# Second product of the expert network in three float32r passes, with its low halves from GpSimd

## Chip, cores and metric

One core of one Trainium2 chip. Metric: device time of one execution in microseconds (us), median of several runs.

## The reference

For 16 samples x[b] of 128 x 256 (channels by positions) and a context of the same shape:

```python
x = x + xattn(layernorm(x), ctx, ctx, gamma)     # 8 heads of 16 channels, softmax over 256 keys
x = x + ffn(layernorm(x), ...)

def ffn(x):                                       # H = 256
    top_expert = argmax(softmax(x @ Wg.T))
    out0 = gelu(x @ W0a.T + b0a) @ W0b.T + b0b    # hidden size 512
    out1 = relu(x @ W1a.T + b1a) @ W1b.T + b1b
    return where(top_expert == 0, out0, out1)
```

## The kernel before

Everything is float32 to the outside. Each engine runs its own instruction list, written out by hand; semaphores (`wait_ge`, `then_inc`) tie the lists together. All lists share one loop: `for n in range(-LEAD, SLOTS)` with LEAD = 7 and SLOTS = 64. A slot is one pair of heads of one sample: `b, j = divmod(n, 4)`, and `c, k = divmod(n + 7, 4)` is the sample whose row maxima are taken ahead.

**Attention.** q and k are split into a high part (ScalarE, `high`, rounded to float32r) and a low part (GpSimd, `low`); SP stacks them by DMA into `qkst` (`stacks`, 6 DMAs of 128 KB a sample). In each slot TensorE does the scores of sample b (`scores`, L654, into `st`) and the scores in the other layout for sample c (`maxima`, L642, into `smax`); ScalarE takes exp of `st` (`exp`, L513); VectorE takes the negated row maxima of `smax` (`take_max`, L358). `st` and `smax` have one buffer each: scores wait for the exp before, maxima for the take_max before. Once per sample the maxima are transposed, split (`copy_max`, `max_parts`) and put into `qkst` by two small DMAs (`max_rows`, L190); the first scores of that sample wait for them. `values` (32 matmuls, L666), `transpose_od` and `transpose_att` finish the attention. VectorE then makes x1 (`residual`), its moments, x_norm and the gate; GpSimd takes the inverse root (`rstd`, L239) and the expert masks.

**Expert network.** It runs on pairs of samples, i = 0 to 7, four samples behind the attention. A pair takes eight slots: an even and an odd value of b. There are 8 units of 128 hidden features: 0 to 3 are gelu, 4 to 7 relu. The first product (`gemm1`, L723) is already in three float32r passes: w high by x high, w high by x low, w low by x high, 6 matmuls of 256 columns a unit for both samples. The weights' high half is made by ScalarE (L576) and the low half by GpSimd (L309) at b = 2 and 3. `hidden` (L542) applies gelu or relu from PSUM bank `ff[:, u // 2 % 2]` into `hid`. The second product (`gemm2`, L740) multiplies `hid` by `w2t` in float32, 8 units a sample, in `ff[:, b % 2]`. `final` (L418 and L423) masks the two experts' outputs, adds x1 and makes y, and `gemm1` waits for y before it writes the same banks.

By slots, with b even: j = 0 gemm1 units 0 to 3; j = 1 the gelu units on ScalarE, behind exp; j = 2 gemm1 units 4 to 7 and the relu units; j = 3 gemm2 of sample b - 4, units 0 to 3. With b odd: j = 0 gemm2 of sample b - 5, units 4 to 7; j = 2 and 3 gemm2 of sample b - 4. `final` of the even sample stands on VectorE at j = 2 of odd b, that of the odd sample at j = 0 of the next even b, behind take_max. The first pair is at b = 4 and 5; the last two pairs of products (samples 12 to 15) stand behind the loop. Pairs 0 to 5 are in the loop.

**Start.** SP loads the samples, issues the stacks and the max rows, and in its iterations b = 0 and b = 1 also w1 and w2 (L225, L227).

Of the kernel before, what the change touches and what calls it, by code (L numbers as in the profile page):

```python
# [16 lines left out]
EXPERTS = 2  # L17
# [13 lines left out]
ROWS = STACK + 2  # L31
STACK_INC = 2 * len(Q_PART) * 16
# [13 lines left out]
X1 = 8  # L46


def build(nc, first, qkin, xvin, w1, w2, b1, b2, wg, gamma, out):
    with ExitStack() as stack:  # L50
# [28 lines left out]
        w2t = sb("w2t", [128, UNITS, L])  # L79
        b1t = sb("b1t", [128, UNITS])  # L80
# [8 lines left out]
        bias_r = sb("bias_r", [128, EXPERTS * L])  # L89
# [22 lines left out]
        hid = sb("hid", [128, UNITS, 2 * C])  # L112
        yt = sb("yt", [128, 2, L])
# [27 lines left out]
        s_g1, s_hid, s_g2 = sem("s_g1"), sem("s_hid"), sem("s_g2")  # L141
        s_y0, s_y = sem("s_y0"), sem("s_y")
# [21 lines left out]
        def _(sp):  # L164
# [50 lines left out]
            for b in range(B):  # L215
# [20 lines left out]
        def _(pool):  # L236
# [54 lines left out]
            for n in range(-LEAD, SLOTS):  # L291
                b, j = divmod(n, PAIRS)
                for c in prepared(n):
                    if c > 2:
                        rstd(c, mv1, c, s_var1, s_rstd1)
                    low(c)
# [8 lines left out]
                if j == 2 and b >= 2:  # L305
                    masks(b - 2)
                if b == 3 and j < LC:
# [8 lines left out]
        def _(dve):  # L316
# [96 lines left out]

            def final(b):
# [11 lines left out]
            def gate_and_bias(step):  # L426
# [6 lines left out]
                if step == 2:  # L433
                    dve.wait_ge(s_bias, 1)
                    dve.tensor_tensor(bias_r[:, :], bias_f[:, :], bias_p[:, 0, :], ALU.subtract).then_inc(s_bias, 1)
                if step == 3:
                    dve.wait_ge(s_bias, 2)
                    dve.tensor_copy(bias_p[:, 1, :], bias_r[:, :]).then_inc(s_bias, 1)
                if step == 4:
                    dve.wait_ge(s_bias, 3)  # L440
                    dve.tensor_tensor(bias_p[:, 2, :], bias_r[:, :], bias_p[:, 1, :], ALU.subtract).then_inc(s_bias, 1)
# [15 lines left out]
            for n in range(-LEAD, SLOTS):  # L457
                b, j = divmod(n, PAIRS)
                c, k = divmod(n + LEAD, PAIRS)
                if c == 0:  # L460
# [11 lines left out]
                if j == 0 and b >= 2:  # L472
                    if b >= 6 and b % 2 == 0:
                        final(b - 5)
# [27 lines left out]
        def _(act):  # L502
# [33 lines left out]

            def hidden(i, u):
                if u % 2 == 0:
                    act.wait_ge(s_g1, UNITS // 2 * i + u // 2 + 1)
                if u == 0 and i:  # L540
# [24 lines left out]
            for n in range(-LEAD, SLOTS):  # L565
                b, j = divmod(n, PAIRS)
                c, k = divmod(n + LEAD, PAIRS)
                if b >= 1:
# [12 lines left out]
                if j == 1 and b >= 4:  # L581
                    if b % 2 == 0:
                        if b == 4:
                            act.wait_ge(s_small, 64)
                        for u in range(4):
                            hidden((b - 4) // 2, u)
# [5 lines left out]
                if j == 3 and b >= 2:  # L592
                    high_xT(b - 2)
            for u in range(4):
# [10 lines left out]
        def _(pe):  # L605
# [121 lines left out]

            def gemm2(b, units):
                t = b % 2
                if 0 in units:  # L730
                    if b == 0:
                        pe.wait_ge(s_w2, 16)
                        pe.wait_ge(s_bias, 7)
                        pe.wait_ge(s_ones, 2)
                    pe.wait_ge(s_hid, UNITS * (b // 2) + (UNITS if t else UNITS - 2))
# [106 lines left out]
```

## Time and profile before

| | |
|---|---|
| Median of 3 runs | 268.23 us (266.91 to 270.09) |
| The profiled execution | 267.05 us |
| its span (first to last instruction) | 264.8 us |
| TensorE, weight loads, VectorE, ScalarE, GpSimd busy | 86%, 65%, 63%, 51%, 24% |
| mean granted TensorE clock | 0.972 of 2.4 GHz |
| HBM read, written | 11.28 MB, 2.10 MB |

The busy share by 40 slices of 6.6 us shows the three stages: a start of some 70 us in which TensorE is often idle and the DMA engines are full, pairs of samples to 230 us with TensorE at 9 tenths, and a tail.

```profile
PE   0748947869599999999999999999999989989995
...
DVE  3775687989635787578757875787476615333302
ACT  2014335665249454945494549554944494632230
...
DMA  4589999989712447375837582646202000000101
```

Each digit is tenths of a slice. Spans of matmuls overlap, so a busy TensorE need not be at its peak; the starts of matmuls tell its rate.

### The profile page before, as it was taken

How to read it: one execution, taken by the hardware profiler on the slowest of the kernel's cores; microseconds unless marked ns; L12 is line 12 of the kernel's file. 1: busy time of each engine (PE TensorE's matmuls, PEld its weight loads, DVE VectorE, ACT ScalarE, POOL GpSimd, SP SyncE). 2: the span in 40 equal slices, each digit the busy share in tenths (PEclk: the TensorE clock that was granted, in tenths of full speed). 3: DMA queues.
4: the chain of work that ended last, by engine and by line, in shares of the span. 5: the costliest groups of instructions: out<-in, count | busy, mean ns of one | idle time of the engine just before them, and what ended most of it. 6: DMA issues, size and time to landing. Idle time of an engine off the chain costs nothing.

```text
span 264.8 us, 4862 instructions
## 1 busy us (share of the span) xinstructions
PE 228.1 (86%) x1858; PEld 172.2 (65%) x1872; DVE 167.5 (63%) x348; ACT 134.7 (51%) x208; POOL 63.9 (24%) x112
## 2 busy tenths in 40 slices
PE   0748947869599999999999999999999989989995
PEld 0425524444478676867686768676867676869893
DVE  3775687989635787578757875787476615333302
ACT  2014335665249454945494549554944494632230
POOL 6592120335700431043104310431101011011000
PEclk9999999798779999999999999999999999999999
DMA  4589999989712447375837582646202000000101
GB/s 158 85 156 165 207 289 171 253 165 153 102 22 80 101 136 110 100 107 123 116 101 102 125 117 62 99 97 108 64 0 64 0 22 2 20 22 0 40 2 40
DMA packets 19562, 25.75 MB, mean 97 GB/s; under 512 B 2644, under 2 KB 13140, under 8 KB 19284
## 3 DMA queue, kind: packets, MB, share of 16 engines
q1 hardware_dynamic: 18312, 24.25, 46.7%
q10 hardware_dynamic: 1228, 1.19, 2.1%
q8 instruction: 15, 0.25, 0.5%
q14 instruction: 7, 0.06, 0.1%
HBM read 11.28 MB, written 2.10 MB: 51 GB/s over the span
## 4 chain that ended last, share of the span: by engine, by line
PE 58%; ACT 17%; DVE 9%; DMA 7%; issue 7%; POOL 0%; SPq 0%; ACTq 0%; DVEq 0%
PE ff L740 21%; PE ff L723 12%; PE st L654 8%; DMA qkst<-mlow 6%; PE od L666 6%; ACT P L513 5%; ACT hid L542 4%; PE smax L642 3%; ACT L542 3%; PE st L629 2%; PE od L674 2%; ACT L513 2%; DVE nmax L351 2%; DVE y L423 1%; DVE yt L418 1%
## 5 line engine op out<-in xcount | busy, mean ns | idle before, releaser
L513 ACT ACTIVATE P<-st 128x1024 f32<-128x1024 f32 x64 | 65.8, 1028 | 85.4 <-PE st L654 76.9
L358 DVE TENSOR_REDUCE nmax<-smax 128x4 f32<-128x1024 f32 x54 | 66.2, 1226 | 40.2 <-PE smax L642 38.9
L740 PE MATMUL ff<-w2t,hid 128*128 128x256 f32 x256 | 60.0, 379 | 1.5 <-issue 1.1
L740 PEld LDWEIGHTS ff<-w2t,hid 128*128 128x128 f32 x256 | 47.7, 190 | 5.8
L723 PE MATMUL ff<-xnTh,w1h 128*128 128x256 f32 x128 | 39.1, 306 | 9.0 <-DVE y L423 3.4
L239 POOL TENSOR_TENSOR mv<-mv,power 128x1 f32<-128x1 f32 x31 | 18.3, 591 | 103.8 <-DVE mv L323 103.8
L654 PE MATMUL st<-qkst 50*128 50x256 f32 x240 | 31.2, 339 | 9.1 <-DMA qkst<-mlow 5.5
L723 PE MATMUL ff<-xnTl,w1h 128*128 128x256 f32 x128 | 37.1, 290 | 0.0
L723 PE MATMUL ff<-xnTh,w1l 128*128 128x256 f32 x128 | 37.1, 290 | 0.0
L654 PEld LDWEIGHTS st<-qkst 50*128 50x128 f32 x240 | 18.5, 191 | 26.2 <-issue 14.4
L666 PE MATMUL od<-P,vt 128*32 128x256 f32 x512 | 33.5, 406 | 0.0
L723 PEld LDWEIGHTS ff<-xnTh,w1h 128*128 128x128 f32 x128 | 25.2, 197 | 12.1 <-DVE y L423 4.4
L244 POOL TENSOR_TENSOR parts<-qk,parts 128x512 fp32r<-128x512 f32 x14 | 17.8, 1274 | 62.1 <-ACT parts L507 62.0
L542 ACT ACTIVATE hid<-ff,b1t 128x256 f32<-128x256 f32 x64 | 25.5, 479 | 9.7 <-PE ff L723 9.6
L723 PEld LDWEIGHTS ff<-xnTl,w1h 128*128 128x128 f32 x128 | 25.3, 197 | 0.0
L723 PEld LDWEIGHTS ff<-xnTh,w1l 128*128 128x128 f32 x128 | 25.2, 197 | 0.0
L666 PEld LDWEIGHTS od<-P,vt 128*32 128x32 f32 x512 | 15.8, 117 | 14.0 <-issue 6.0
L642 PE MATMUL smax<-qkst 48*128 48x256 f32 x216 | 24.2, 304 | 0.0
L642 PEld LDWEIGHTS smax<-qkst 48*128 48x128 f32 x216 | 18.2, 203 | 2.5 <-issue 1.3
L418 DVE SCALAR_TENSOR_TENSOR yt<-ff,mask,x 128x256 f32<-128x256 f32 x16 | 7.6, 474 | 11.5 <-PE ff L740 11.5
L412 DVE TENSOR_TENSOR xnTl<-tr,xnTh 128x256 fp32r<-128x256 f32 x16 | 6.7, 421 | 11.7 <-ACT xnTh L534 11.7
L507 ACT ACTIVATE parts<-qk 128x512 fp32r<-128x512 f32 x14 | 8.9, 639 | 9.0 <-DVE qk L347 9.0
(73 smaller groups left out, 250.9 us busy)
## 6 DMA issues: line engine op xcount, KB each, us to landing
qkst<-parts SPq DMA_DIRECT2D x87, 128.0 KB, 4.7
xv<-in_xv SPq DMA_DIRECT2D x16, 256.0 KB, 2.9
qk<-in_qk SPq DMA_DIRECT2D x15, 256.0 KB, 4.6
out<-y SPq DMA_DIRECT2D x16, 128.0 KB, 2.4
w1t<-in_w SPq DMA_DIRECT2D x1, 1024.0 KB, 10.2
w2t<-in_w SPq DMA_DIRECT2D x1, 1024.0 KB, 9.9
qkst<-parts ACTq DMA_DIRECT2D x3, 128.0 KB, 6.2
qk<-in_first SPq DMA_DIRECT2D x1, 256.0 KB, 3.4
```

The lines of the kernel that those rows point to most:

```text
L239: pool.tensor_tensor(mv[:, b % 2, 11:12], mv[:, b % 2, 10:11], power[:, 0:1], ALU.pow).then_inc(s_rstd, 1)
L244: pool.tensor_tensor(parts[:, c % 2, 0:4:3, :], qk[:, place(c, QK), :, :], parts[:, c % 2, 1:3, :], ALU.subtract).then_inc(s_lo, 1)
L358: dve.tensor_reduce(nmax[:, c % 2, :, :, j].rearrange("p a e -> p e a"), (ff if c in WIDE and j % 2 else smax)[:, :, :, :], AX.X, ALU.max, ...
L418: dve.scalar_tensor_tensor(out=yt[:, t, :], in0=ff[:, t, 0, :], scalar=mask[:, b % X1, 0:1], in1=x1[:, b % X1, :], op0=ALU.mult, op1=ALU.a ...
L507: act.activation(parts[:, c % 2, 1:3, :], qk[:, place(c, QK), :, :], ACT.Copy).then_inc(s_hi, 1)
L513: act.activation(P[:, b % 2, j, :, :, :].rearrange("p e a l -> p (e a l)"), st[:, :, :, :].rearrange("p e a l -> p (e a l)"), ACT.Exp, sca ...
L542: act.activation(hid[:, u, :], ff[:, u // 2 % 2, u % 2, :], ACT.Gelu if u < HM else ACT.Relu, bias=b1t[:, u:u + 1]).then_inc(s_hid, 1)
L642: mm = pe.matmul((ff if wide and j % 2 else smax)[:, e, a, :], qkst[rows, s, j, 0, a * 128:(a + 1) * 128], qkst[rows, s, j, 1, :], start=T ...
L654: mm = pe.matmul(st[:, e, a, :], qkst[rows, s, j, 1, a * 128:(a + 1) * 128], qkst[rows, s, j, 0, :], start=True, stop=True)
L666: mm = pe.matmul(od[32 * j:32 * j + 32, e * L:(e + 1) * L], vt[:, b % 2, HEADS * a + PAIRS * e + j, :], P[:, b % 2, j, e, a, :], start=a = ...
L723: mm = pe.matmul(ff[:, u // 2 % 2, u % 2, :], w[:, a, e, m * 128:(m + 1) * 128], xs[:, i % 2, a, :], start=a == 0 and n == 0, stop=a == LC ...
L740: mm = pe.matmul(ff[:, t, u // HM, :], hid[:, u, t * C:(t + 1) * C], w2t[:, u, :], start=False, stop=u == UNITS - 1)
```

## The change

For samples 0 to 11 (the six pairs in the loop) the second product goes in three float32r passes too. `hid` is split as x and w1 are: the high half of the gelu units by VectorE (`high_gelu`, a copy to float32r of 128 x 1024), that of the relu units by ScalarE (`high_relu`), both low halves by GpSimd (`low_hidden`, a subtraction of 128 x 1024 each). w2 is split in the same way at b = 3. A unit has three matmuls: hid high by w2 high and by w2 low (`high_pass`), hid low by w2 high (`low_pass`). The four samples behind the loop keep `gemm2` in float32.

Order, beside that: the gelu units stand ahead of exp in their slot on ScalarE; `final` of the odd sample stands ahead of take_max on VectorE; `low` of q and k stands two slots later on GpSimd; the even sample's last low pass, and so its final sum, comes in slot j = 2 of odd b. w1 and w2 are loaded by DMAs that ScalarE issues at n = 0 and n = 4. Buffers: X1 goes from 8 to 6, bias_r is gone; two new tiles for w2 and two for hid.

```diff
@@ SP
-                if b == 0:
-                    sp.dma_start(w1t[:, :, :, :].rearrange("p a e f -> p (a e f)"), w1).then_inc(s_w1, 16)
-                if b == 1:
-                    sp.dma_start(w2t[:, :, :].rearrange("p u l -> p (u l)"), w2).then_inc(s_w2, 16)
@@ GpSimd
+            def low_hidden(i, e):
+                pool.wait_ge((s_hidHg, s_hidHr)[e], i + 1)
+                units = slice(e * HM, (e + 1) * HM)
+                pool.tensor_tensor(hidL[:, units, :], hid[:, units, :], hidH[:, units, :], ALU.subtract).then_inc(s_hidL, 1)
...
+                if j == 0 and b >= 5 and b % 2:
+                    low_hidden((b - 5) // 2, 1)
+                if b >= 4 and j == 3 and b % 2 == 0:
+                    low_hidden((b - 4) // 2, 0)
+                for c in prepared(n - 2 if n > 0 else n) if n else ():
                     low(c)
...
+                if b == 3 and j >= 2:
+                    pool.wait_ge(s_w2h, j - 1)
+                    half = slice((j - 2) * HM, (j - 1) * HM)
+                    pool.tensor_tensor(w2l[:, half, :], w2t[:, half, :], w2h[:, half, :], ALU.subtract).then_inc(s_w2l, 1)
@@ VectorE
+            def high_gelu(i):
+                dve.wait_ge(s_hid, UNITS * i + HM)
+                if i:
+                    dve.wait_ge(s_g2, 2 * i)
+                dve.tensor_copy(hidH[:, 0:HM, :], hid[:, 0:HM, :]).then_inc(s_hidHg, 1)
...
+                if j == 0 and b >= 6 and b % 2 == 0:
+                    final(b - 5)
                 if c == 0:
                     take_max0(k)
...
+                if j == 2 and b >= 4 and b % 2 == 0:
+                    high_gelu((b - 4) // 2)
@@ ScalarE
+            def high_relu(i):
+                act.wait_ge(s_hid, UNITS * (i + 1))
...
+                act.activation(hidH[:, HM:UNITS, :], hid[:, HM:UNITS, :], ACT.Copy).then_inc(s_hidHr, 1)
...
+                if j == 1 and b >= 4:
+                    if b % 2 == 0:
...
+                        for u in range(4):
+                            hidden((b - 4) // 2, u)
                 if b >= 1:
                     exp(b, j)
...
+                if n == 0:
+                    act.dma_start(w1t[:, :, :, :].rearrange("p a e f -> p (a e f)"), w1).then_inc(s_w1, 16)
+                if n == PAIRS:
+                    act.dma_start(w2t[:, :, :].rearrange("p u l -> p (u l)"), w2).then_inc(s_w2, 16)
...
+                if b == 3 and j < 2:
+                    act.wait_ge(s_w2, 16)
+                    half = slice(j * HM, (j + 1) * HM)
+                    act.activation(w2h[:, half, :], w2t[:, half, :], ACT.Copy).then_inc(s_w2h, 1)
@@ TensorE
+            def high_pass(b, e):
+                pe.wait_ge((s_hidHg, s_hidHr)[e], b // 2 + 1)
...
+                for u in range(e * HM, (e + 1) * HM):
+                    for w in (w2h, w2l):
+                        pe.matmul(ff[:, t, e, :], hidH[:, u, t * C:(t + 1) * C], w[:, u, :], start=False, stop=False)
+            def low_pass(b, e):
+                pe.wait_ge(s_hidL, EXPERTS * (b // 2) + e + 1)
...
                 if j == 0:
...
                     if odd:
-                        gemm2(b - 5, range(4, 8))
+                        low_pass(b - 5, 0)
+                        high_pass(b - 5, 1)
                 if j == 2:
...
                     if odd:
-                        gemm2(b - 4, range(0, 4))
+                        low_pass(b - 5, 1)
+                        begin(b - 4)
+                        high_pass(b - 4, 0)
+                        low_pass(b - 4, 0)
...
                 if j == 3 and b >= 1:
...
                     if even:
-                        gemm2(b - 4, range(0, 4))
+                        begin(b - 4)
+                        high_pass(b - 4, 0)
                     if odd:
-                        gemm2(b - 4, range(4, 8))
+                        high_pass(b - 4, 1)
+                        low_pass(b - 4, 1)
```

`hidden` also waits for hidL of the pair before instead of s_g2, which lets it overwrite `hid` earlier; `begin` is the bias matmul that stood in gemm2.

Three places as the instructions stand there. First TensorE, the odd sample's first slot, behind its maxima (b = 7; od<-identf,attT is a transpose of the attention's output). Before:

```order
L642 MATMUL smax<-qkst 128x256 [waits s_max]
L642 MATMUL smax<-qkst 128x256 x3
L681 MATMUL od<-identf,attT 128x128 [waits s_attT]
L681 MATMUL od<-identf,attT 128x128
L740 MATMUL ff<-w2t,hid 128x256 x2
L740 MATMUL ff<-w2t,hid 128x256 [waits s_hid]
L740 MATMUL ff<-w2t,hid 128x256
```

And now:

```order
L688 MATMUL smax<-qkst 128x256 [waits s_max]
L688 MATMUL smax<-qkst 128x256 x3
L727 MATMUL od<-identf,attT 128x128 [waits s_attT]
L727 MATMUL od<-identf,attT 128x128
L796 MATMUL ff<-w2h,hidL 128x256 [waits s_hidL]
L796 MATMUL ff<-w2h,hidL 128x256 x3
L790 MATMUL ff<-w2h,hidH 128x256 [waits s_hidHr]
L790 MATMUL ff<-w2l,hidH 128x256
```

Four float32 units, of which the first two wait for nothing new, gave way to a low pass of the gelu units that waits for GpSimd (s_hidL) and a high pass of the relu units that waits for ScalarE (s_hidHr).

Second ScalarE, the second slot of an even sample (b = 6); P<-st is exp, mhigh<-tr the transposed maxima's high part. Before:

```order
L513 ACTIVATE P<-st 128x1024 [waits s_sc]
L525 ACTIVATE mhigh<-tr 8x256 [waits s_mT,s_mst0]
L542 ACT_TABLE_LOAD [waits s_g2]
L542 ACTIVATE hid<-ff,b1t 128x256 [waits s_g1]
L542 ACTIVATE hid<-ff,b1t 128x256
L542 ACTIVATE hid<-ff,b1t 128x256 [waits s_g1]
L542 ACTIVATE hid<-ff,b1t 128x256
L513 ACT_TABLE_LOAD
L513 ACTIVATE P<-st 128x1024 [waits s_sc]
L530 ACTIVATE ods<-od 128x512 [waits s_pv]
```

And now:

```order
L578 ACT_TABLE_LOAD [waits s_hidL]
L578 ACTIVATE hid<-ff,b1t 128x256 [waits s_g1]
L578 ACTIVATE hid<-ff,b1t 128x256
L578 ACTIVATE hid<-ff,b1t 128x256 [waits s_g1]
L578 ACTIVATE hid<-ff,b1t 128x256
L538 ACT_TABLE_LOAD
L538 ACTIVATE P<-st 128x1024 [waits s_sc]
L550 ACTIVATE mhigh<-tr 8x256 [waits s_mT,s_mst0]
L538 ACTIVATE P<-st 128x1024 [waits s_sc]
L555 ACTIVATE ods<-od 128x512 [waits s_pv]
```

Table load, four units and the load back moved from between two exps to ahead of both; the first load waits for s_hidL in place of s_g2.

Third GpSimd at b = 3, from the slot j = 0; parts<-qk,parts is `low`, vt<-xv a padded copy of v. Before:

```order
L239 TENSOR_TENSOR mv<-mv,power 128x1 [waits s_var2]
L309 TENSOR_TENSOR w1l<-w1t,w1h 128x1024 [waits s_w1h]
L239 TENSOR_TENSOR mv<-mv,power 128x1 [waits s_var1]
L244 TENSOR_TENSOR parts<-qk,parts 128x2x256 [waits s_hi]
L309 TENSOR_TENSOR w1l<-w1t,w1h 128x1024 [waits s_w1h]
L257 COPY vt<-xv 128x16x16 [waits s_pv,s_xv0]
L262 TENSOR_SCALAR mask<-lead 128x1 [waits s_lead]
L262 TENSOR_SCALAR mask<-lead 128x1
```

And now:

```order
L241 TENSOR_TENSOR mv<-mv,power 128x1 [waits s_var2]
L326 TENSOR_TENSOR w1l<-w1t,w1h 128x1024 [waits s_w1h]
L241 TENSOR_TENSOR mv<-mv,power 128x1 [waits s_var1]
L326 TENSOR_TENSOR w1l<-w1t,w1h 128x1024 [waits s_w1h]
L259 COPY vt<-xv 128x16x16 [waits s_pv,s_xv0]
L270 TENSOR_SCALAR mask<-lead 128x1 [waits s_lead]
L270 TENSOR_SCALAR mask<-lead 128x1
L323 TENSOR_TENSOR w2l<-w2t,w2h 128x1024 [waits s_w2h]
L246 TENSOR_TENSOR parts<-qk,parts 128x2x256 [waits s_hi]
L323 TENSOR_TENSOR w2l<-w2t,w2h 128x1024 [waits s_w2h]
```

`low` went from ahead of the second half of w1l to behind the masks, and the two halves of w2l came in around it.

## Rows read from the trace of the kernel before

**Rows 1.** The page: busy time by engine; the chain that ended last, by engine.
```profile
PE 228.1 (86%) x1858; PEld 172.2 (65%) x1872; DVE 167.5 (63%) x348; ACT 134.7 (51%) x208; POOL 63.9 (24%) x112
...
PE 58%; ACT 17%; DVE 9%; DMA 7%; issue 7%; POOL 0%; SPq 0%; ACTq 0%; DVEq 0%
```

**Rows 2.** Chain of waits, whole span: start us, length us, what was being worked on.
```profile
101.04 1.71 PE ff L723 x12
...
207.56 1.71 PE ff L723 x12
```

**Rows 3.** Timeline of TensorE, one pair: start us, length us, engine, line, operation, count.
```profile
126.95 0.28 PE L723 MATMUL ff<-xnTh,w1l 128*128 128x256 f32 x1
127.68 0.39 PE L723 MATMUL ff<-xnTh,w1h 128*128 128x256 f32 x1 [0.45 <-DVE y L423]
...
129.32 0.51 PE L654 MATMUL st<-qkst 50*128 50x256 f32 x4
...
132.17 0.50 PE L654 MATMUL st<-qkst 50*128 50x256 f32 x4
132.51 0.40 PE L642 MATMUL smax<-qkst 48*128 48x256 f32 x4
133.34 0.39 PE L723 MATMUL ff<-xnTh,w1h 128*128 128x256 f32 x1 [0.43 <-ACT hid L542]
...
136.29 0.38 PE L706 MATMUL tr<-identf,xn 128*128 128x128 f32 x2
...
137.98 1.89 PE L740 MATMUL ff<-w2t,hid 128*128 128x256 f32 x8
139.80 0.51 PE L654 MATMUL st<-qkst 50*128 50x256 f32 x4
```

**Rows 4.** Timeline of ScalarE, the same pair.
```profile
131.15 1.28 ACT L542 ACT_TABLE_LOAD   x1
132.45 1.57 ACT L542 ACTIVATE hid<-ff,b1t 128x256 f32<-128x256 f32 x4
134.03 1.28 ACT L513 ACT_TABLE_LOAD   x1
135.33 1.03 ACT L513 ACTIVATE P<-st 128x1024 f32<-128x1024 f32 x1
```

**Rows 5.** Timeline of VectorE, the same pair.
```profile
137.39 1.23 DVE L358 TENSOR_REDUCE nmax<-smax 128x4 f32<-128x1024 f32 x1 [2.57 <-PE smax L642]
```

**Rows 6.** Groups by line, shapes apart: count, busy us, mean ns, idle before.
```profile
L740 PEld LDWEIGHTS ff<-w2t,hid 128*128 128x128 f32 x256 | 47.7, 190 | 5.8
...
L309 POOL TENSOR_TENSOR w1l<-w1t,w1h 128x1024 fp32r<-128x1024 f32 x2 | 4.7, 2349 | 0.0
...
L397 DVE TENSOR_SCALAR xn<-x,mv 128x256 f32<-128x256 f32 x16 | 7.2, 447 | 2.1 <-POOL mv L239 2.1
...
L438 DVE CAST bias_p<-bias_r 128x512 bf16<-128x512 f32 x1 | 0.6, 634 | 0.0
```

**Rows 7.** Chain of waits, the first 76 us.
```profile
30.85 5.37 DMA qkst<-mlow
...
41.01 5.61 DMA qkst<-mlow
...
68.16 2.51 issue
70.67 5.40 PE ff L723 x24
```

**Rows 8.** Timeline of GpSimd (POOL), the first 76 us.
```profile
61.01 2.36 POOL L309 TENSOR_TENSOR w1l<-w1t,w1h 128x1024 fp32r<-128x1024 f32 x1
...
68.23 2.34 POOL L309 TENSOR_TENSOR w1l<-w1t,w1h 128x1024 fp32r<-128x1024 f32 x1
```

**Rows 9.** Timeline of VectorE (DVE), the first 76 us.
```profile
62.52 1.00 DVE L397 TENSOR_SCALAR xn<-x,mv 128x256 f32<-128x256 f32 x1
```

**Rows 10.** One stretch of 2 us by engine, with clock, DMA share, GB/s.
```profile
36.00:38.00 2.00, 1.22 (x8) 0.93 (x8) 0.83 (x2) 0.90 (x1) 0.61 (x2) 1.00 1.02 419
```

More of the change, by code:

```diff
@@ L31 @@
 ROWS = STACK + 2
+LAST = B // 2 - 2
 STACK_INC = 2 * len(Q_PART) * 16
@@ L45 @@
 XV = 4
-X1 = 8
+X1 = 6
 def build(nc, first, qkin, xvin, w1, w2, b1, b2, wg, gamma, out):
@@ L79, in build @@
         w2t = sb("w2t", [128, UNITS, L])
+        w2h = sb("w2h", [128, UNITS, L], F32R)
+        w2l = sb("w2l", [128, UNITS, L], F32R)
         b1t = sb("b1t", [128, UNITS])
@@ L88, in build @@
         bias_f = sb("bias_f", [128, EXPERTS * L])
-        bias_r = sb("bias_r", [128, EXPERTS * L])
         bias_p = sb("bias_p", [128, 3, EXPERTS * L], BF16)
@@ L112, in build @@
         hid = sb("hid", [128, UNITS, 2 * C])
+        hidH = sb("hidH", [128, UNITS, 2 * C], F32R)
+        hidL = sb("hidL", [128, UNITS, 2 * C], F32R)
         yt = sb("yt", [128, 2, L])
@@ L141, in build @@
         s_g1, s_hid, s_g2 = sem("s_g1"), sem("s_hid"), sem("s_g2")
+        s_hidHg, s_hidHr, s_hidL, s_w2h, s_w2l = map(sem, ("s_hidHg", "s_hidHr", "s_hidL", "s_w2h", "s_w2l"))
         s_y0, s_y = sem("s_y0"), sem("s_y")
@@ L472, in _ @@
                 if j == 0 and b >= 2:
-                    if b >= 6 and b % 2 == 0:
-                        final(b - 5)
                     residual(b - 2)
@@ L535, in high_xT @@
                                ACT.Copy).then_inc(s_xTh, 1)
+            def high_relu(i):
+                act.wait_ge(s_hid, UNITS * (i + 1))
+                if i:
+                    act.wait_ge(s_g2, 2 * i)
+                act.activation(hidH[:, HM:UNITS, :], hid[:, HM:UNITS, :], ACT.Copy).then_inc(s_hidHr, 1)
             def hidden(i, u):
@@ L539, in hidden @@
                     act.wait_ge(s_g1, UNITS // 2 * i + u // 2 + 1)
-                if u == 0 and i:
+                if u % HM == 0 and 0 < i < LAST:
+                    act.wait_ge(s_hidL, EXPERTS * (i - 1) + u // HM + 1)
+                if u == 0 and i == LAST:
+                    act.wait_ge(s_hidL, EXPERTS * LAST)
+                if u == 0 and i > LAST:
                     act.wait_ge(s_g2, 2 * i)
@@ L567, in _ @@
                 c, k = divmod(n + LEAD, PAIRS)
+                if j == 1 and b >= 4:
+                    if b % 2 == 0:
+                        if b == 4:
+                            act.wait_ge(s_small, 64)
+                        for u in range(4):
+                            hidden((b - 4) // 2, u)
                 if b >= 1:
@@ L580, in _ @@
                     copy_max(c - 1)
[L581 to L586, printed above, removed]
                 if j == 2 and b >= 1:
@@ L593, in _ @@
                     high_xT(b - 2)
+                    if b >= 4 and b % 2 == 0:
+                        high_relu((b - 4) // 2)
             for u in range(4):
@@ L726, in gemm1, with begin @@
                     mm.then_inc(s_g1, 1)
+            def begin(b):
+                t = b % 2
+                if b == 0:
+                    pe.wait_ge(s_w2, 16)
+                    pe.wait_ge(s_bias, 7)
+                    pe.wait_ge(s_ones, 2)
+                pe.wait_ge(s_hid, UNITS * (b // 2) + (UNITS if t else UNITS - 2))
+                pe.matmul(ff[:, t, :, :], onesb[:, :], bias_rows[:, :], start=True, stop=False)
+            def high_pass(b, e):
+                t = b % 2
+                pe.wait_ge((s_hidHg, s_hidHr)[e], b // 2 + 1)
+                if b == 0:
+                    pe.wait_ge(s_w2l, EXPERTS)
+                for u in range(e * HM, (e + 1) * HM):
+                    for w in (w2h, w2l):
+                        pe.matmul(ff[:, t, e, :], hidH[:, u, t * C:(t + 1) * C], w[:, u, :], start=False, stop=False)
+            def low_pass(b, e):
+                t = b % 2
+                pe.wait_ge(s_hidL, EXPERTS * (b // 2) + e + 1)
+                for u in range(e * HM, (e + 1) * HM):
+                    mm = pe.matmul(ff[:, t, e, :], hidL[:, u, t * C:(t + 1) * C], w2h[:, u, :],
+                                   start=False, stop=u == UNITS - 1)
+                if e == EXPERTS - 1:
+                    mm.then_inc(s_g2, 1)
             def gemm2(b, units):
@@ L730, in gemm2 @@
                 if 0 in units:
[L731 to L735, printed above, removed]
-                    pe.matmul(ff[:, t, :, :], onesb[:, :], bias_rows[:, :], start=True, stop=False)
+                    begin(b)
                 for u in units:
```

6 lines of the change are left out of this document (3 added, 3 removed).

## Prediction, written before the changed kernel ran

> **What bounds the kernel now.** I read the page first. TensorE is busy for 86% of the span and carries 58% of the chain that ended last; no other engine has over 63% [rows 1]. An average over stages does not say where a saving counts, so I next read the chain in order of time. From 101.04 to 207.56 us it shows the same pattern four times, once per pair of samples: 106.5 / 4 = 26.63 us a pair [rows 2]. Two further pairs, at b = 4, 5 and b = 14, 15, have nearly the same pattern; ahead of them lies a start of 70 us, behind them a tail of 35 us.
>
> Inside one pair I read TensorE's timeline [rows 3] by starts, because its spans overlap. Let T be the start of the even sample's first scores. A pair reaches from T to the next T, and the odd sample of this pair begins at 139.80 us. TensorE stands still in two places only. Before the matmul at 127.68 it waits for y, the final sum of the odd sample before: the previous start is 126.95 and starts are 0.12 apart, so 0.61 us are lost (0.45 by the profile's own count). Before 133.34 it waits for the first gelu units: from 132.51 the four maxima take 0.33 us, so 0.50 are lost. All else is back to back. So in these pairs nearly every microsecond taken from TensorE is a microsecond of the span, as long as the other engines keep up.
>
> **The second product.** Before, a block of four units in float32 takes from 137.98 to 139.80, 1.82 us or 0.455 us a unit [rows 3]. A pair has four such blocks (two samples of eight units), 7.28 us. In three float32r passes a unit costs three matmuls of the form that the first product has already: 24 of them take from 133.34 to 136.29, 0.123 us each [rows 3], 0.369 us a unit. 48 matmuls are 5.90 us. Saving: 1.4 us a pair; I take 1.3, as the float32 blocks that a transpose follows are a little shorter than 1.82.
>
> The Trainium skill ("FP8 and Floating Point Precision", TensorE Precision Notes) says that true FP32 takes 4 passes through the array. By that rule three passes cost three quarters, 0.341 us for 0.455, and the pair would save 1.8 us instead of 1.4. No row here has 0.114 us for a float32r matmul; the sum goes by 0.123.
>
> **The gelu units ahead of exp.** At the even sample's second slot ScalarE now does load table, four gelu units, load table, and only then the exp that the next scores wait for. Before, the exp came first. The first load now hides behind the first product. With the wait for y gone, the first product's last unit ends 0.61 us sooner, so the scores of row 129.32 start at 128.71 and the units 2 and 3 can be taken from about 128.9. Two units are half of 1.57 [rows 4], 0.79; load and start-up 1.30 (134.03 to 135.33); exp 1.03: done at 132.03. TensorE wants to start the next scores 0.61 us ahead of 132.17, at 131.56. It waits until 132.07. So the wait for y mostly becomes a wait for exp: of 0.61 us 0.10 is left. The wait of 0.50 before 133.34 goes, since units 0 and 1 are long done. Both together: 0.6 us a pair.
>
> **The new operations and their cover.** Per pair and expert there is one copy to the high half and one subtraction, of 128x1024.
> - ScalarE's copy (relu half): an exp of this size is 1.03 us [rows 4]. It stands after the last exp and xnTh of the even sample, and I place its end at 139.6, some 1.2 us after TensorE starts the odd sample. The high pass that needs it starts after scores, maxima, a transpose and a low pass, 1.4 us after that start. It just fits; if it is 0.5 us late, TensorE loses 0.3.
> - VectorE's copy (gelu half): VectorE stands idle for 2.57 us at that place, its next maximum waiting for the first product to pass [rows 5]. A cast of half the size takes 0.634 us [rows 6], so this one 1.27 at most, and it costs nothing. Without that cover it would be 1.2 us a pair.
> - GpSimd's two subtractions: 2.35 us each [rows 6], 4.7 us a pair on an engine at 24% [rows 1]. Gelu half: starts about 135.9, done 138.3, needed in the odd sample's first slot. Relu half: done about 142.0, needed at 144.3, two slots on. Both are covered, the first by 1 us. Behind them in GpSimd's queue stand the low halves of sample c (needed six slots on) and a one-column power for layer norm, which VectorE reads 1.5 us later.
> - VectorE's final sum now stands ahead of take_max in the even slot. It waits only for the pass just issued, and its 1 us delays a maximum that no one waits for there.
>
> Walking the pair with these numbers gives 24.7 us for 26.6: gain 1.9 a pair (1.3 + 0.6). The four pairs between the rows 2 and the pair b = 14, 15 give 5 x 1.9 = **9.5 us**. The last four samples keep the float32 form and the tail moves as it is.
>
> **The first pair.** It has no wait for y, and its table load must wait for the first product, so exp costs more: gain 1.3 + 0.5 - 0.8 = **1.0 us**.
>
> **The start.** Four things change.
> - Before, TensorE waits 2.51 us at 68.16 [rows 7]. That wait, which the chain calls issue, is for w1l: GpSimd's second half ran 68.23 to 70.57, queued behind the low halves of a sample that themselves waited for ScalarE [rows 8]. Now the low halves come later in the queue, the second half starts at about 64 and ends before TensorE asks. Gain 2.5.
> - Moved, it runs beside VectorE's TENSOR_SCALAR over 128x256. In the first half's time such an op took 1.00 us, where the mean of its group is 0.447 [rows 6], and it ended just after GpSimd did [rows 8, 9]. Now the normalising of q meets that, and ScalarE has two w2h copies of 1.03 more. Together up to 0.9 us on the chain through attT. Loss 0.9.
> - The loads of w1 and w2, 1 MB each, go on ScalarE's queue, about 5 us before their old places. At 419 GB/s one takes 2.5 us [rows 10]. The small max rows wait behind what is in flight: 5.37 and 5.61 us from issue to landing [rows 7], so w1 now delays the first of them by up to 2.5 us and w2 the second. But the same megabyte is gone from the time after it, when SP's queue was full as well, and by the third max rows most is given back. I take 1.2 lost; bounds 0 and 2.9.
> - After the 2.5 us of idling the 24 matmuls at 70.67 ran 0.213 us apart, 5.40 us in all [rows 7], for 2.95 at full clock [rows 3]: the granted clock had fallen to 1.2 GHz. Without the idle time I expect about half of that, 1.1 us; bounds 0 and 2.4.
>
> Start: 2.5 - 0.9 - 1.2 + 1.1 = **1.5 us**.
>
> On the queues the Trainium skill ("DMA: Bandwidth & Descriptors", DMA queue model) says that each DMA engine round-robins between the rows of queues, so ScalarE's queue does not stand behind SP's. No run here shows it. Strictly FIFO service would make the cost 0 and the time 1.2 us less.
>
> **Sum.** 9.5 + 1.0 + 1.5 = 12.0 us. The profiled execution took 267.05 us; that makes 255.05. The median of the runs shown is 1.2 us above it, so 256.2 against the median. I give 255.5.
>
> **Rivals.**
> - *The start keeps its gain or loses more.* With DMA free and the clock up the sum is 12 + 1.2 + 1.3 + 0.9, about 15.4: 252 us. With 2.9 lost, no clock regained and another 1.5 from idle gaps it is 7.7: 260 us. For the second speaks that the DMA engines have nothing idle even while the big loads run: their share is 1.02 [rows 10]. Chance 0.12 each.
> - *The subtraction arrives late in each pair.* If hidL or hidH comes 1 us later than I placed it, say because the gelu order pushes ScalarE's chain past the odd sample's start, five pairs give back 5 to 6 us: 261 us. Against: covers of 1 us and more in three of four places. Chance 0.10.
> - *The other side: weight loads.* A float32 unit has two weight loads, the three passes have three, and a load's span is 190 ns [rows 6]. If loads did not hide behind matmuls of 256 columns, a unit would cost 3 x 0.19 = 0.57 for 0.455, and 96 units lose 11 us for the 7.8 gained: 268 + 11 - (12 - 7.8) = 275 us. It decides from 0.5 us a unit on, at which the other gains are used up. Against: the first product has the same loads and comes out at 0.123. Chance 0.03.
> - *The change does little*, because VectorE takes over: it is at 63% of the span [rows 1], but in the odd sample I count 10.8 us of work for it from its timeline, against 11.0 for TensorE. If each of its slots were 0.4 us longer the pair would stay near 26.3 and the time near 264. Chance 0.03.
>
> **Numbers.** My forecast, 253 to 259 us, has 0.60. Time 255.5, range 251 to 261. A measurement of this kernel tells about 1% from no change: 2.7 us. Faster by over 1% 0.94, within 1% 0.02, slower 0.04.
>
> **What would show it.** Starts of equal matmuls 24.7 us apart from pair to pair. Each high pass of eight matmuls about 0.98 us. No wait for y before unit 2 of the first product; a wait of about 0.5 us for exp before the even sample's third scores. No 2.5 us gap before the first product; w1l's second half ending by 67 us. The first max rows landing 2 us later. Wrong would be: waits of TensorE on hidL or hidH, a lower granted clock inside the pairs, or float32r matmuls further apart than 0.13 us.

## The result, and the profile after

The changed kernel takes 256.85 us (median of 4, 256.7 to 258.24) against 268.5 us for the kernel before (median of 4): ratio 0.956, 95% interval 0.952 to 0.960. The profiled execution took 256.82 us (before 267.05), its span 255.0 us (before 264.8). The forecast was 255.5, range 251 to 261. The total is right; inside it one stage came out with the other sign.

The page after has a line of busy times and one of the chain by engine, like [rows 1]:

```profile
PE 221.7 (87%) x1968; PEld 171.4 (67%) x1968; DVE 170.5 (67%) x354; ACT 143.6 (56%) x216; POOL 97.0 (38%) x126
...
PE 71%; DVE 10%; ACT 8%; DMA 5%; issue 4%; POOL 0%; DVEq 0%; ACTq 0%
```

GpSimd has gone from 64 to 97 us of work and still stands nowhere on the chain; TensorE's part of the chain rose from 58% to 71%. The work was moved to an engine that had room.

Where the 9.8 us of span come from is read by the start of TensorE's scores (L654 before, L700 now), which close every stage:

| stage (b = sample) | before | after | gained | forecast |
|---|---|---|---|---|
| start, to the second scores of b = 4 | 76.00 | 76.35 | -0.35 | 1.5 |
| first pair, to b = 6 | 22.07 | 21.53 | 0.5 | 1.0 |
| four pairs, b = 6 to 14 | 106.52 | 99.16 | 7.4 | 7.6 |
| last pair and tail, from b = 14 | 60.2 | 58.0 | 2.2 | 1.9 |

**Inside a pair.** The chain of waits after, to be read against [rows 2] (start us, length us): the same group of 24 matmuls stands at

```profile
99.00 2.85 PE ff L769 x24
...
173.38 2.85 PE ff L769 x24
```

with two more between, so (173.38 - 99.00) / 3 = 24.79 us a pair, for 26.63 before. TensorE's timeline after, at the places of [rows 3] (start us, length us, then what it waited for, if anything):

```profile
126.36 0.28 PE L769 MATMUL ff<-xnTh,w1l 128*128 128x256 f32 x1
126.57 0.50 PE L700 MATMUL st<-qkst 50*128 50x256 f32 x4
...
129.91 0.50 PE L700 MATMUL st<-qkst 50*128 50x256 f32 x4 [0.42 <-ACT P L538]
...
137.14 0.73 PE L796 MATMUL ff<-w2h,hidL 128*128 128x256 f32 x4
137.70 0.28 PE L790 MATMUL ff<-w2h,hidH 128*128 128x256 f32 x1
...
138.54 0.28 PE L790 MATMUL ff<-w2l,hidH 128*128 128x256 f32 x1
138.75 0.50 PE L700 MATMUL st<-qkst 50*128 50x256 f32 x4
...
142.27 0.73 PE L796 MATMUL ff<-w2h,hidL 128*128 128x256 f32 x4
```

The waits for y and for hid are gone, one for exp has come, and eight matmuls of the high pass lie 0.12 apart (137.70 to 138.54 is seven steps). Their operands, as the timelines of ScalarE, VectorE and GpSimd show them for this pair:

```profile
136.15 1.08 ACT L566 ACTIVATE hidH<-hid 128x1024 fp32r<-128x1024 f32 x1
...
132.49 0.67 DVE L435 CAST hidH<-hid 128x1024 fp32r<-128x1024 f32 x1
...
133.25 2.39 POOL L265 TENSOR_TENSOR hidL<-hid,hidH 128x1024 fp32r<-128x1024 f32 x1 [2.48 <-DVE hidH L435]
...
137.33 2.39 POOL L265 TENSOR_TENSOR hidL<-hid,hidH 128x1024 fp32r<-128x1024 f32 x1
```

The gelu low half is done at 135.64 and needed at 137.14 (cover 1.5 us); the relu low half at 139.72 and needed at 142.27 (2.5 us); ScalarE's high half at 137.2 and needed at 137.70. That last cover, 0.5 us, is the thin one.

**The start.** The chain of waits over the first 85 us, against [rows 7]:

```profile
31.37 8.42 DMA qkst<-mlow
...
73.42 1.59 PE ff L769 x12
...
81.07 3.04 PE ff L769 x24
```

The issue of 2.51 us (a wait of TensorE, for w1l) has gone, and so has the second DMA of 5.61; but the first is 8.42 us long in place of 5.37. The first product ran at full clock: this stretch view has us, busy us by engine (TensorE, weight loads, VectorE, ScalarE, GpSimd), granted clock, DMA share, GB/s.

```profile
70.00:76.00 6.00, 5.45 (x44) 4.42 (x45) 5.51 (x11) 4.05 (x6) 6.00 (x7) 1.00 0.35 106
```

VectorE and GpSimd in the same stretch, against [rows 8, 9]:

```profile
67.31 0.99 DVE L414 TENSOR_SCALAR xn<-x,mv 128x256 f32<-128x256 f32 x1
...
70.20 0.97 DVE L364 TENSOR_SCALAR qk<-qk,mv 128x256 f32<-128x256 f32 x1
```

```profile
65.80 2.36 POOL L326 TENSOR_TENSOR w1l<-w1t,w1h 128x1024 fp32r<-128x1024 f32 x1
...
68.67 2.36 POOL L326 TENSOR_TENSOR w1l<-w1t,w1h 128x1024 fp32r<-128x1024 f32 x1
```

The three samples behind the first rows show a second loss. From the first scores of b = 1 to those of b = 4 they take 10.67, 10.83 and 10.27 us, for 10.41, 10.46 and 9.41 before: 1.5 us more in all, although no scores of b = 2 and 3 wait for max rows any more. The values blocks (32 matmuls between a sample's second and third scores) grew from 2.77, 2.73 and 2.67 us to 3.58, 3.28 and 3.25, 1.9 us in all. The block of b = 3 as a stretch, columns as above, before and after:

```profile
60.53:63.20 2.67, 2.67 (x33) 1.15 (x32) 2.60 (x6) 0.52 (x2) 2.67 (x2) 0.68 1.16 122
```

```profile
65.02:68.27 3.25, 3.25 (x33) 1.38 (x32) 3.17 (x7) 1.00 (x2) 3.00 (x3) 0.56 1.16 123
```

The granted clock is 0.56 where it was 0.68 (at b = 2, 0.55 for 0.67); at a clock of 1.00, inside the pairs, the same block takes 1.87 us. And ahead of that block TensorE now waits for VectorE's maximum:

```profile
64.07 0.50 PE L688 MATMUL smax<-qkst 48*128 48x256 f32 x4 [0.55 <-DVE nmax L375]
```

### The profile page after: what moved, and what is told of

Same layout as the page of the kernel before. It is cut to its first block, busy times and chain, and to the rows that moved or that the text cites. A ratio compares the mean times of both kernels' runs of the same rounds, so it can differ in the third digit from the quotient of the medians.

```text
span 255.0 us, 5113 instructions
## 1 busy us (share of the span) xinstructions
PE 221.7 (87%) x1968; PEld 171.4 (67%) x1968; DVE 170.5 (67%) x354; ACT 143.6 (56%) x216; POOL 97.0 (38%) x126
## 4 chain that ended last, share of the span: by engine, by line
PE 71%; DVE 10%; ACT 8%; DMA 5%; issue 4%; POOL 0%; DVEq 0%; ACTq 0%
PE ff L769 17%; PE od L712 9%; PE ff L790 9%; PE st L700 9%; PE ff L796 5%; PE ff L808 5%; PE smax L688 5%; ACT P L538 4%; DMA qkst<-mlow 3%; PE od L720 3%; DVE nmax L375 3%; PE st L675 2%; ACT hid L578 2%; PE od L727 2%; DVE nmax L368 2%
## 5 line engine op out<-in xcount | busy, mean ns | idle before, releaser
L700 PE MATMUL st<-qkst 50*128 50x256 f32 x240 | 31.3, 340 | 13.2 <-ACT P L538 6.7
L769 PE MATMUL ff<-xnTh,w1h 128*128 128x256 f32 x128 | 37.5, 293 | 1.2 <-DVE y L446 1.2
L700 PEld LDWEIGHTS st<-qkst 50*128 50x128 f32 x240 | 18.7, 193 | 27.9 <-ACT P L538 10.2
L578 ACT ACTIVATE hid<-ff,b1t 128x256 f32<-128x256 f32 x64 | 26.8, 471 | 16.7 <-PE ff L769 16.5
L769 PE MATMUL ff<-xnTl,w1h 128*128 128x256 f32 x128 | 35.9, 281 | 0.0
L265 POOL TENSOR_TENSOR hidL<-hid,hidH 128x1024 fp32r<-128x1024 f32 x12 | 28.6, 2387 | 18.5 <-DVE hidH L435 14.1
L712 PE MATMUL od<-P,vt 128*32 128x256 f32 x512 | 35.5, 424 | 0.0
L790 PE MATMUL ff<-w2h,hidH 128*128 128x256 f32 x96 | 26.6, 310 | 0.0
L688 PE MATMUL smax<-qkst 48*128 48x256 f32 x216 | 24.2, 304 | 0.9 <-DVE nmax L375 0.8
L769 PEld LDWEIGHTS ff<-xnTl,w1h 128*128 128x128 f32 x128 | 24.1, 188 | 0.0
L790 PE MATMUL ff<-w2l,hidH 128*128 128x256 f32 x96 | 23.9, 283 | 0.0
L688 PEld LDWEIGHTS smax<-qkst 48*128 48x128 f32 x216 | 18.0, 201 | 3.5 <-issue 1.8
L790 PEld LDWEIGHTS ff<-w2l,hidH 128*128 128x128 f32 x96 | 18.2, 190 | 0.3
L790 PEld LDWEIGHTS ff<-w2h,hidH 128*128 128x128 f32 x96 | 18.1, 189 | 0.1
```

The source lines that it names most:

```text
L265: pool.tensor_tensor(hidL[:, units, :], hid[:, units, :], hidH[:, units, :], ALU.subtract).then_inc(s_hidL, 1)
L578: act.activation(hid[:, u, :], ff[:, u // 2 % 2, u % 2, :], ACT.Gelu if u < HM else ACT.Relu, bias=b1t[:, u:u + 1]).then_inc(s_hid, 1)
L688: mm = pe.matmul((ff if wide and j % 2 else smax)[:, e, a, :], qkst[rows, s, j, 0, a * 128:(a + 1) * 128], qkst[rows, s, j, 1, :], start=T ...
L700: mm = pe.matmul(st[:, e, a, :], qkst[rows, s, j, 1, a * 128:(a + 1) * 128], qkst[rows, s, j, 0, :], start=True, stop=True)
L712: mm = pe.matmul(od[32 * j:32 * j + 32, e * L:(e + 1) * L], vt[:, b % 2, HEADS * a + PAIRS * e + j, :], P[:, b % 2, j, e, a, :], start=a = ...
L769: mm = pe.matmul(ff[:, u // 2 % 2, u % 2, :], w[:, a, e, m * 128:(m + 1) * 128], xs[:, i % 2, a, :], start=a == 0 and n == 0, stop=a == LC ...
```

## Experiments

The theory after this reading had three parts. In the pairs, the product gives about 1.1 us, and the two orders (gelu units ahead of exp, final sum ahead of the maximum) each about 0.7. In the start, the two weight loads issued early take away what the missing issue gives. And GpSimd's order, not the loads, removed that issue. The rivals: the second queue as such delays the small rows; one of the orders is worth nothing; the product brings all of it. All kernels are the changed one with one part edited; ratios are to the kernel before of the same batch, against 0.956 for the changed kernel.

### Weight loads back on SP's queue

```diff
-                if n == 0:  act.dma_start(w1t ..., w1)
-                if n == PAIRS:  act.dma_start(w2t ..., w2)
+                if b == 0:  sp.dma_start(w1t ..., w1)      # behind load_xv(b + 2)
+                if b == 1:  sp.dma_start(w2t ..., w2)
```

> The changed kernel with the loads of w1 and w2 back on SP's queue at b = 0 and b = 1. Changed kernel: ratio to before 0.956, span 255.0 us. Theory A (from the changed kernel's trace: the first max rows land 8.42 us after their issue, against 5.37 before, and TensorE never gets the time back; its landmarks at the third and fourth sample stay 3.7 us late): span 251.3 us, ratio 0.943, first max rows within 5.6 us, and waits for max rows again at the second and third sample. Theory B (prediction's term: the delay is mostly given back, 1.2 us lost): span 253.8, ratio 0.952. Theory C (the delay is in the number of DMA bytes before the row, not the queue, and moves to the next sample): span 255, ratio 0.956.

Measured: 255.42 us, ratio 0.950 [0.943, 0.956], span 254.2. Chain of waits:

```profile
31.43 6.09 DMA qkst<-mlow
...
42.32 5.85 DMA qkst<-mlow
...
53.52 5.37 DMA qkst<-mlow
```

The first max rows take 2.3 us less than in the changed kernel, but now the slots wait for the second and third too, as before. Of the lead (first scores of b = 4 at 69.54 for 71.61) most is lost again in the first product: two stretches, columns as above,

```profile
70.00:72.00 2.00, 1.64 (x11) 1.36 (x10) 1.97 (x5) 1.17 (x2) 2.00 (x2) 0.68 0.23 80
72.00:74.00 2.00, 2.00 (x12) 2.00 (x11) 1.47 (x5) 0.00 (x0) 2.00 (x2) 0.50 0.43 104
```

show a granted clock of 1.2 GHz, and the second scores of b = 4 come 6.02 us behind the first, for 4.74. In the 3 us ahead of that product TensorE's longest wait is 0.24 us. So the span is only 0.8 us shorter, and this run alone does not tell the place in time from the queue.

### The same loads later, still on ScalarE's queue

```diff
-                if n == 0:
+                if n == 2:
                     act.dma_start(w1t ..., w1)
-                if n == PAIRS:
+                if n == PAIRS + 2:
                     act.dma_start(w2t ..., w2)
```

> The changed kernel with the same two loads still on ScalarE's queue, but two slots later (n = 2 and n = 6), behind the issue of the max rows. If the place in time is what costs (theory A): first max rows land within 5.6 us again, span 251 to 252, ratio 0.943 to 0.947, like the run with SP's queue. If it is the second queue itself that delays SP's packets: the first max rows land in time, but the second ones, whose stacks share the DMA engines with w1, land 2.5 us late, span 254 to 255, ratio 0.952 to 0.956.

Measured: 253.41 us, ratio 0.945 [0.938, 0.951], span 251.0. The issue of w1 moved from 25.9 to 32.0 us, that of w2 from 40.7 to 44.1. The chain of waits and the stretch with the first product:

```profile
31.00 5.66 DMA qkst<-mlow
```

```profile
68.00:72.00 4.00, 3.61 (x30) 3.21 (x29) 3.49 (x9) 2.11 (x3) 4.00 (x3) 1.00 0.27 70
```

This is the run that decides. The queue is the same as in the changed kernel, only the time differs, and the first rows take 2.8 us less. All four of the microseconds are in the start: the second scores of b = 4 stand at 72.34 for 76.35, and all later stages are equal to within 0.05 us. In the run before this one w1 went out at 32.5 us, from the other queue, and the rows took 6.09. So the time of issue costs, not the queue. An early issue from SP's queue was not tried. (0.4 of the four are a first load of 3.56 us for 3.93, which no edit touches.)

The lead also grows after the first rows, from 3.1 us at b = 1 to 4.0 at b = 3. All of that 0.9 is in the values blocks of b = 1 to 3, which take 9.20 us together for 10.11; for b = 3 the granted clock is 0.61 for 0.56. The w2 load is 3.4 us later too, and I did not take the two apart.

### GpSimd's low halves of q and k at their old place

```diff
+                    if n < 15:
+                        low(c)       # behind the power of sample c, as before
...
-                for c in prepared(...): low(c)
+                for c in prepared(...):
+                    if n > 16:
+                        low(c)
```

> The changed kernel with GpSimd's low halves of q and k, up to b = 3, back in their old slot, ahead of the second half of w1l. Theory A: TensorE waits about 2.5 us before its first product again and the 24 matmuls behind that wait run 0.213 us apart (granted clock at 1.2 GHz), so the span is 4.2 us longer: 259.2 us, ratio 0.972. Theory B: with ScalarE's copies of w2 and the later start the wait is there, but the clock stays up: 2.0 us longer, 257, ratio 0.963. Theory C: w1l is not what TensorE waited for: no change.

Measured: 260.78 us, ratio 0.972 [0.965, 0.979], span 260.9. Chain of waits:

```profile
74.94 2.52 issue
77.46 5.47 PE ff L772 x24
```

The wait of [rows 7] comes back to 0.01 us and the half clock with it: 5.47 us for 24 matmuls. Two terms of the start, 2.5 and the clock, hang on this one reorder, and it is not the weight loads that brought them. The run also prices the meeting of VectorE and GpSimd, for here the normalising of q has GpSimd idle beside it:

```profile
71.91 0.40 DVE L367 TENSOR_SCALAR qk<-qk,mv 128x256 f32<-128x256 f32 x1
```

It takes 0.40 us where the changed kernel takes 0.97. Yet the sample of b = 3 is as long as there (10.31 us for 10.27), and TensorE is ready for its first product 1.61 us after the first scores of b = 4 (73.33 to 74.94), where it is 1.70 us in the changed kernel (71.61 to 73.31). So the meeting costs 0.1 us. (The first max rows of this run took 9.06 us to land, 0.6 more than in the changed kernel; that is no part of the reorder's price.)

### The final sum behind the maximum again

```diff
-                if j == 0 and b >= 6 and b % 2 == 0:
-                    final(b - 5)           # ahead of take_max
...
                 if j == 0 and b >= 2:
+                    if b >= 6 and b % 2 == 0:
+                        final(b - 5)
                     residual(b - 2)
```

> The changed kernel with the final sum of the odd sample back behind take_max on VectorE. Theory A: the wait for y of 0.6 us a pair returns ahead of unit 2 of the first product, and the wait for exp (0.42 us a pair) stays, since exp moves with the units: 5 x 0.6 = 3.0 us longer, span 258.0, ratio 0.967. Theory B: the wait for exp absorbs it, since exp is then the later of the two: 0.5 to 1 us longer, ratio 0.958 to 0.960.

Measured: 260.60 us, ratio 0.971 [0.964, 0.977], span 257.9. Timeline of TensorE:

```profile
125.01 0.28 PE L769 MATMUL ff<-xnTh,w1l 128*128 128x256 f32 x1
125.74 0.38 PE L769 MATMUL ff<-xnTh,w1h 128*128 128x256 f32 x1 [0.45 <-DVE y L446]
...
130.68 0.50 PE L700 MATMUL st<-qkst 50*128 50x256 f32 x4 [0.42 <-ACT P L538]
```

From 125.01 to 125.74 is 0.73 us where 0.12 is the step: 0.61 lost, as in [rows 3]. The wait for exp stays as it was. A pair is 25.48 us, 0.69 more. In the prediction I had let the wait for y turn into most of a wait for exp; it does not, the two now simply add.

### The gelu units behind exp again

```diff
-                if j == 1 and b >= 4:  ... hidden((b - 4) // 2, u) for u in 0..3   # ahead of exp
                 if k == 0 and 2 <= c <= B:
                     copy_max(c - 1)
+                if j == 1 and b >= 4:  ... the same block, behind exp and copy_max
```

> The changed kernel with the first four units back behind exp and the maxima's copy on ScalarE, final sum still ahead of take_max. Changed kernel: 0.956, span 255.0. Theory A (by the prediction's reckoning): the wait for exp of 0.42 us a pair goes and the wait for the first gelu units of 0.5 returns, so even there; but ScalarE is 0.4 us later at the relu half's copy and TensorE waits for hidHr or for the odd sample's exp: 0.5 us a pair longer in all, span 257.5 to 258, ratio 0.966. Theory B: the cover at the relu half's copy holds and nothing changes: span 255.5, ratio 0.958.

Measured: 260.11 us, ratio 0.967 [0.961, 0.972], span 258.5, 25.47 us a pair. TensorE, then ScalarE:

```profile
131.45 0.39 PE L769 MATMUL ff<-xnTh,w1h 128*128 128x256 f32 x1 [0.44 <-ACT hid L578]
...
137.48 0.50 PE L700 MATMUL st<-qkst 50*128 50x256 f32 x4 [0.27 <-ACT P L538]
...
138.34 0.71 PE L796 MATMUL ff<-w2h,hidL 128*128 128x256 f32 x4
139.12 0.39 PE L790 MATMUL ff<-w2h,hidH 128*128 128x256 f32 x1
```

```profile
137.96 1.11 ACT L566 ACTIVATE hidH<-hid 128x1024 fp32r<-128x1024 f32 x1
```

The wait for hid is back and the one of 0.42 for exp is gone; those two nearly cancel. What is left of the 0.68 us is ScalarE's chain behind it. Its relu units now come late, its exp is late by 0.27 at the odd sample's first scores, and its high half ends at 139.07, so that the high pass starts 0.78 us behind the low pass where it was 0.56 (137.14 to 137.70). The gelu order is what keeps the cover of 0.5 us over ScalarE's copy. The prediction had named the price ("if it is 0.5 us late, TensorE loses 0.3") but had put the cover down to the place of the copy, not to the order of the gelu units.

### Both orders as before, with the three passes

```diff
 the last two edits together
```

> The changed kernel with both orders undone: units behind exp, final sum behind take_max. One alone cost 2.9 us of span (final). Theory A: waits as in the kernel before, 0.6 us for y and 0.5 for the first gelu units a pair, and the late relu half: 1.0 to 1.2 us a pair over the changed kernel, span 260.5, ratio 0.978. Theory B, the two are worth the same thing twice: no more than the final sum alone, 258, ratio 0.970.

Measured: 263.58 us, ratio 0.980 [0.974, 0.986], span 261.4. Chain of waits, then timeline of TensorE:

```profile
126.54 1.68 PE ff L769 x12
...
152.71 1.71 PE ff L769 x12
```

```profile
132.18 0.39 PE L769 MATMUL ff<-xnTh,w1h 128*128 128x256 f32 x1 [0.44 <-ACT hid L578]
```

A pair is 26.17 us: 1.38 more than with both, and 0.69 + 0.68 = 1.37 by the two single runs. With this product the orders add up without overlap.

### The second product in float32, orders kept

```diff
-                    for w in (w2h, w2l):
-                        pe.matmul(ff[...], hidH[...], w[:, u, :], ...)
+                    pe.matmul(ff[...], hid[...], w2t[:, u, :], ...)
...
-                for u in ...:  pe.matmul(ff[...], hidL[...], w2h[:, u, :], ...)
```

> The changed kernel with all its splitting of hid and w2, its waits and its order, but the second product of samples 0 to 11 computed in float32 from hid and w2t: each high pass has the four float32 matmuls in place of eight, the low passes have none. Theory A (starts of equal matmuls: 0.455 us for a float32 unit, 3 x 0.120 for the passes): 96 units x 0.09 = 8.6 us longer at most, less what the even sample's shorter low passes leave; span 262 to 263.5, ratio 0.982 to 0.987. Theory B (the passes' gain comes in part from the order): 4 us longer or less, ratio under 0.972.

Measured: 263.10 us, ratio 0.976 [0.970, 0.982], span 261.9. Chain of waits, then timeline of TensorE:

```profile
126.26 2.85 PE ff L769 x24
...
152.15 2.86 PE ff L769 x24
```

```profile
137.69 1.89 PE L789 MATMUL ff<-w2t,hid 128*128 128x256 f32 x8
139.51 0.50 PE L700 MATMUL st<-qkst 50*128 50x256 f32 x4
```

Six pairs use the passes, 6 x 1.09 = 6.5 of the 6.9 us of span. A pair is 25.89 us (152.15 - 126.26), so the passes are worth 1.09 us a pair, where 1.3 was forecast, and the orders with the float32 product 26.63 - 25.89 = 0.74. In the old order the passes are worth only 26.63 - 26.17 = 0.46, with all that the splitting of hid costs. The two parts of the change need each other: alone they make 1.20, together 1.84.

### A unit of the first product in place of the wait for exp

With the weight loads later, as above, and:

```diff
+                if j == 2 and b >= 4 and b % 2 == 0:
+                    gemm1((b - 4) // 2, 4)      # ahead of the even sample's third scores
                 if b >= 1:
                     scores(b, j)
...
-                        for u in range(4, 8):
+                        for u in range(5, 8):
```

> The kernel with the weights' loads later on ScalarE's queue (span 251.0, ratio 0.945), and on TensorE the first product's unit 4 ahead of the even sample's third scores instead of behind them: 0.72 us of work put where TensorE waits 0.42 us a pair for exp (1.07 in the first pair, 0.65 in the last). Theory A: the waits go, nothing else is late: 3.0 to 3.4 us shorter, span 248, ratio 0.933. Theory B: maxima, low half of the maxima and hid's high half all come 0.3 us later and TensorE now waits for the max rows' DMA or for hidL at the odd sample's first slot: under 1 us shorter, ratio 0.941 or more.

Measured: 251.16 us, ratio 0.931 [0.925, 0.937], span 250.5. Timeline of TensorE, then chain of waits:

```profile
126.95 0.28 PE L769 MATMUL ff<-xnTh,w1l 128*128 128x256 f32 x1
127.16 0.51 PE L700 MATMUL st<-qkst 50*128 50x256 f32 x4
```

```profile
120.63 2.84 PE ff L769 x24
145.13 2.84 PE ff L769 x24
```

The scores come without a wait, and a pair is 24.50 us for 24.79: 0.29 for a wait counted at 0.42, as a block of matmuls cut in two pays for its second start (the slot that gets unit 4 grows from 3.34 us, wait included, to 3.76, and the next one shrinks by 0.7). The first pair gains 0.7 (20.83 for 21.54). Of the three versions this is the fastest, 5.7 us below the changed kernel by medians of two batches. Its span is still above the one expected: the fill gave 2.4 us (0.7 in the first pair, 4 x 0.29, 0.5 behind b = 14) where the waits counted make 3, and its start was 1.9 us slower than in the run with the loads alone (74.19 for 72.34); the first load took 4.18 us there, for 3.56, and the rows 6.18, for 5.66. The same code stands in both up to that point, so that part is spread from execution to execution: 1.1 us in these two transfers, and 0.7 in the samples b = 1 to 3, whose values blocks take 9.99 us for 9.20. The profile shows no cause for it.

## Why the prediction held, and where it did not

- **The pair, 24.7 forecast, 24.79 measured.** Right in the sum; the parts were both off, and cancel. The product was put at 1.3 and is 1.09. The matmuls are as fast as assumed (0.12 apart), but 48 of them are cut into five pieces, and each piece pays for its start and its end: 137.70 to 138.75 is 1.05 us where eight steps are 0.96, and the low pass at 137.14 takes 0.56 for four steps of 0.12. The waits were put at 0.6; the orders are worth 0.74 with the float32 product.
- **The weight loads' rivals.** L790's weight loads are as long as those of [rows 6] and lie under the matmuls; the case of 275 us is excluded, and so is VectorE as the bound: it is 67% busy, and TensorE's maxima (L688) wait 0.8 us for it in the whole span.
- **The rule of four passes.** The Trainium skill ("FP8 and Floating Point Precision", TensorE Precision Notes) gave 1.8 us a pair for three passes in place of four. The runs show 1.09. The trace does not agree with that ratio: three float32r matmuls at 0.119 are 0.357 us, against 0.455 for the float32 unit and 0.341 by the rule, and the cuts between blocks take the rest.
- **Subtractions and copies.** Placed right within 0.5 us where they end; VectorE's cast took 0.67 us, half the bound of 1.27. GpSimd's two cost nothing, as said.
- **The first pair, 1.0 forecast, 0.5 measured.** The wait for exp is 1.07 us there, where 0.8 was set, and the product gives 0.2 less.
- **The start, gain 1.5 forecast, loss 0.35 measured.** The wait for w1l is gone (2.5 forecast and measured). The clock gave 2.3 and not 1.1: the 24 matmuls take 3.04 us for 5.33, at a clock of 1.00 for 0.51 before. "Without the idle time I expect about half of that" was a hedge with no row behind it. The third experiment brings wait and half clock back together; but in the first one 13 of the 24 matmuls run at half clock without the wait, so the wait is not all that decides it. VectorE held by GpSimd was put at 0.9 and cost 0.1: the operation grows from 0.40 to 0.97 us as forecast, but TensorE's way to the first product grows by 0.1 only (third experiment), and nothing on that way waits for ScalarE's copies of w2.
- **The step that failed** is "by the third max rows most is given back. I take 1.2 lost; bounds 0 and 2.9". It measured 4.5 us, far outside its bounds. The first rows took 3.05 us more (8.42 for 5.37), a little over the whole bound, and in place of something given back the three samples behind them took 1.5 us more. Two things that the prediction did not have stand there. The engines' own chain is nearly as long as the one with the DMA: if the values blocks were as short as before, the three samples would take 29.8 us for 30.3 (an estimate from the lengths above), so only 0.5 could have come back. And those blocks ran longer at a lower granted clock, by 1.9 us. One reading was off too: w1 is issued 6.0 us ahead of its old place (25.9 for 31.9), as said, but w2 only 1.4 (40.7 for 42.1).
- **The sum of the start** is then 2.5 + 2.3 - 0.1 - 4.5 - 0.5 = -0.3 us, where the last 0.5 is a first load of 3.93 us for 3.39, which this change does not touch. Against the forecast the DMA term is 3.3 us worse, the clock 1.2 and VectorE 0.8 better. That they cancel down to an error of 1.85 us is luck; the time of 255.5 is right because the pairs are, and those are right by their mechanism, but for the cover on ScalarE that hangs on the gelu order. Later loads bring 4.0 us of span back (3.6 without the first load).
- **Queues.** The Trainium skill ("DMA: Bandwidth & Descriptors", DMA queue model) has each DMA engine take turns between queues. The trace agrees: from 30 to 34 us 105 packets of ScalarE's queue moved beside 76 of SP's, and 1 MB from ScalarE's queue, issued 5.5 us ahead of the rows from SP's, made these 3.05 us later. With the load issued at 32.0 us no packet of ScalarE's queue moved between 32 and 36 us, and the rows were there at 36.7.

What stays open: whether the w2 load has a part in the 0.9 us by which the lead grows behind the first rows, and what sets the granted clock in the start. It falls in the first product with the loads on SP's queue, though TensorE had no idle stretch of 2 us ahead of it, and it moves over the values blocks from run to run. Each kernel has one trace, so differences of half a microsecond in the start are not sure.

## What to carry to other kernels

A big transfer with slack has a latest place as well as an earliest: issue it right behind the small transfer that something waits for, not ahead of it, whatever queue it is on. Do not credit a stage with "given back later" before having read how long it is without its wait, and at which clock. A slower instruction is not a slower chain: VectorE's operation more than doubled here and cost 0.1 us. And where a new operation fits into a gap, look for what made the gap: here the copy on ScalarE fits only because of the order that the same change gives the gelu units, so either part alone looks poor.

## What the runs showed of the hardware

- A float32r matmul of 256 columns every 0.119 us, and a float32 block of four units (8 matmuls) in 1.82 us; each switch to another block costs TensorE some 0.1 to 0.2 us more than its step. Fewer, longer blocks would be worth a few tenths of a us a pair, an estimate that no run here tries.
- The clock of the 24 matmuls behind 2.5 us without work was 1.2 GHz for all of them (0.213 us apart, 5.33 to 5.47 us in two kernels). At 2.4 GHz they take 3.1. Wait and clock together cost 4.7 there. In the run with the loads on SP's queue 13 of the 24 were as far apart without such a wait.
- The values block of 32 matmuls takes 1.87 us at a granted clock of 1.00, 3.25 at 0.56 and 2.67 at 0.68.
- VectorE's TENSOR_SCALAR of 128x256 takes 0.39 to 0.41 us alone and 0.97 to 1.00 beside GpSimd's 2.36 us subtraction, in three places of two kernels, while a TENSOR_REDUCE (1.23 us at 69.06), a SCALAR_TENSOR_TENSOR (0.47 at 138.20) and a BATCH_NORM_STATS2 (0.43 at 138.71) beside such a subtraction are not held.
